# A pause in the gathers around each block that is selected by one-hots, and the selection moved to the head of its step

## What is computed

```
x_i, x_j = x[dst], x[src]
h = relu(concat(x_i, x_j - x_i) @ W1 + b1)     # 64
h = relu(h @ W2 + b2)                          # 128
h = relu(h @ W3 + b3)                          # 64
m = h @ W4 + b4                                # 32
s, cnt = segment_sum(m, dst), segment_sum(1, dst)
out = layernorm(x + s / max(cnt, 1))
```

## Time and profile before

| what | value |
|---|---|
| median of 3 runs | 2409.53 us (2392.46 to 2433.17) |
| profiled execution, span | 2441.1 us |
| TensorE (PE) busy, 13131 matmul records | 1767.5 us, 72% |
| weight loads (PEld) | 1040.0 us |
| VectorE busy | 947.9 us, 39% |
| ScalarE busy | 602.6 us, 25% |
| GpSimd (POOL) busy | 1125.9 us, 46% |
| DMA | 283.06 MB, mean 116 GB/s |

### The profile page before, as it was taken

How to read it: one execution, slowest core, us unless ns; L and a number is a source line. 1 busy time by engine, 2 the same in 40 slices (tenths; PEclk the granted TensorE clock), 3 DMA queues, 4 the chain that set the end, 5 groups by cost and what they waited for, 6 DMA issues and landing times.

```text
span 2441.1 us, 39243 instructions
## 1 busy us (share of the span) xinstructions
PE 1767.5 (72%) x13131; PEld 1040.0 (43%) x13131; DVE 947.9 (39%) x3086; ACT 602.6 (25%) x945; POOL 1125.9 (46%) x1165
## 2 busy tenths in 40 slices
PE   3133777777768777878787778786867778777797
PEld 2112444444444444444444444444444444444454
DVE  3663343333333343333333333443333333333356
ACT  2233122222212222212222222222221222122234
POOL 5275444453544454354545454544444454444411
PEclk7555787877878787777778877777877877787888
DMA  5334643343434443353434353544344344444332
GB/s 128 98 93 88 200 112 112 106 140 94 136 101 116 126 121 109 103 147 91 135 105 136 104 152 92 152 109 114 104 123 115 111 114 109 133 118 118 109 106 59
DMA packets 189929, 283.06 MB, mean 116 GB/s; under 512 B 84614, under 2 KB 90169, under 8 KB 189156
## 3 DMA queue, kind: packets, MB, share of 16 engines
q1 hardware_dynamic: 152341, 241.67, 33.7%
q0 software_dynamic: 36704, 37.00, 7.3%
q10 hardware_dynamic: 682, 1.85, 0.3%
HBM read 266.51 MB, written 13.73 MB: 115 GB/s over the span
## 4 chain that ended last, share of the span: by engine, by line
PE 63%; issue 23%; another core or an unknown queue 6%; DVE 3%; ACT 2%; DMA 1%; SPq 1%; DVEq 0%; POOL 0%; ACTq 0%; POOLq 0%
PE ps L964 22%; PE ps L996 12%; PE ps L988 10%; PE ps L1019 5%; PE ps L1004 4%; PE ps L919 3%; PE ps L901 3%; PE ps L1016 2%; PE ps L978 2%; ACT work L716 1%; ACT work L731 1%; DMA sums<-in_src 1%; DVE region L1410 0%; DVE region L1292 0%
## 5 line engine op out<-in xcount | busy, mean ns | idle before, releaser
L585 POOL DMA_INDIRECT xj<-z_rows,src_t x1107 | 1074.5, 971 | 1190.9 <-PE ps L919 787.7
L964 PE MATMUL ps<-region,x_p 128*96 128x150 bf16 (+53 forms) x5876 | 569.6, 243 | 416.6 <-issue 407.2
L964 PEld LDWEIGHTS ps<-region,x_p 128*96 128x96 bf16 x5876 | 440.6, 142 | 572.9 <-issue 566.7
L731 ACT ACTIVATE work<-ps,b3s 128x512 f32<-128x512 f32 x196 | 134.7, 687 | 1335.5 <-PE ps L996 1037.1
L996 PE MATMUL ps<-work,w3s 128*64 128x512 f32 x784 | 356.6, 840 | 21.2 <-issue 21.1
L1377 DVE TENSOR_SCALAR region<-region,cst 128x1565 bf16<-128x1565 int16 (+6 forms) x416 | 245.7, 634 | 268.0 <-remote 256.3
L988 PE MATMUL ps<-work,w2s 64*128 64x512 f32 x784 | 298.1, 827 | 6.8 <-ACT work L716 5.6
L724 ACT ACTIVATE work<-ps,b2s 128x512 f32<-128x512 f32 x392 | 250.7, 684 | 161.0 <-PE ps L988 82.7
L1392 DVE COPY work<-ps 128x512 f32<-128x512 f32 x194 | 133.4, 687 | 336.4 <-PE ps L1004 217.0
L1386 DVE CAST work<-ps 96x512 bf16<-96x512 f32 x52 | 35.7, 686 | 513.9 <-PE ps L964 506.8
L1410 DVE TENSOR_SCALAR region<-iota_g,dst_rel 128x42 f32<-128x42 f32 x1120 | 185.7, 250 | 0.0
(11 more groups left out here) (156 smaller groups left out, 826.3 us busy)
## 6 DMA issues: line engine op xcount, KB each, us to landing
dstb<-dst_rows SPq DMA_DIRECT2D x196, 252.0 KB
region<-src_rows SPq DMA_DIRECT2D x104, 391.2 KB
region<-src_rows SPq DMA_DIRECT2D x52, 407.2 KB
region<-src_rows SPq DMA_DIRECT2D x52, 403.2 KB
region<-src_rows SPq DMA_DIRECT2D x52, 376.2 KB
region<-src_rows SPq DMA_DIRECT2D x52, 375.8 KB
region<-src_rows SPq DMA_DIRECT2D x52, 374.0 KB
region<-src_rows SPq DMA_DIRECT2D x52, 366.2 KB
```

Source lines behind the costliest of these rows:

```text
L585: pool.indirect_dma_start(out=xj[:, u, j % UT, j // UT, 0:w], out_offset=None, in_=rows, in_offset=bass.IndirectOffsetOnAxis(ap=cols[:, j: ...
L964: chosen = nc.tensor.matmul(ps[0:XP, XBANK[h], lo - h * UE:hi - h * UE], xb[:, a, :], hot[:, q % QN, at + lo:at + hi], start=not begun[h], ...
```

## The change

A constant `QUIET_LEAD = 1` and a semaphore `s_quiet` are new. `quiet_before(g)` lists the sorted blocks before whose selection GpSimd must stop ahead of batch g: those whose step comes when all batches but one of those issued are used. There GpSimd raises `s_quiet` and waits until all eight chunks of the block are selected. TensorE waits for `s_quiet` before the first matmul of the block, and selects all three parts at the head of the sorted step. The first sorted step is step 11 instead of 7. The steps in which VectorE builds the one-hots and SP loads the lists, and the five and eight buffers, stay.

```diff
--- before.py
+++ after.py
@@ -46,8 +46,9 @@
 LISTS = 2 * SBL * T + 2 * LC
 STEPS = []
 AHEAD = 4
+QUIET_LEAD = 1
 HALF_STEP, PARTS_STEP = 0, 1
-FIRST_SORTED, LAST_SORTED = AHEAD + 3, S_N - 8
+FIRST_SORTED, LAST_SORTED = AHEAD + 7, S_N - 8
 SORTED_AT = [FIRST_SORTED + k * (LAST_SORTED - FIRST_SORTED) // (SB - 1) for k in range(SB)]
 for n in range(S_N):
     k = sum(1 for at in SORTED_AT if at < n)
@@ -290,6 +291,7 @@
                                           sem("windows_of_sources_stored"))
         s_masked, s_maskT, s_maskc = sem("sorted_dst_masked"), sem("sorted_dst_transposed"), sem("sorted_dst_copied")
         s_hot, s_block, s_unit0 = sem("source_onehots"), sem("chunks_selected"), sem("unit0_selected")
+        s_quiet = sem("gathers_paused")
         s_turned = sem("rows_transposed")
         s_x2 = sem("x_in_once_more")
         s_l1 = [sem(f"layer1_unit{n}") for n in range(2)]
@@ -374,6 +376,10 @@
 
         def piece(h):
             return slice(h * NC // XH, (h + 1) * NC // XH)
+
+        def quiet_before(g):
+
+            return [STEPS[s] for s in SSTEP if s - STEPS[s] + QUIET_LEAD == g]
 
         def end_of_pass(eng, off):
             eng.sem_inc(s_arrive, 1)
@@ -574,7 +580,13 @@
             nc.gpsimd.memset(zpad[:, :], 0.0).then_inc(s_set, 1)
             nc.gpsimd.memset(w4s[:, :], 0.0).then_inc(s_w4z, 1)
 
+            def stay_quiet(b):
+                pool.sem_inc(s_quiet, 1)
+                pool.wait_ge(s_block, CN * (b + 1))
+
             def gather(g):
+                for b in quiet_before(g):
+                    stay_quiet(b)
                 u, cols = g % R, src_t[:, g * PT:(g + 1) * PT]
                 rows, w = (x, D) if g < PLAIN else (z_rows, H1)
                 if g == PLAIN:
@@ -948,6 +960,8 @@
                     if b:
                         pe.wait_ge(s_xc[1], b)
                     begun[0] = begun[1] = False
+                if piece == 0:
+                    pe.wait_ge(s_quiet, b + 1)
                 if b == 0 and piece == 0:
                     pe.wait_ge(s_xb, 16)
                     pe.wait_ge(s_maskc, 1)
@@ -1028,7 +1042,8 @@
             def step(s):
                 if s < S_N:
                     if is_sorted(s):
-                        selected_x(s, 2)
+                        for k in range(len(PIECES)):
+                            selected_x(s, k)
                     elif is_plain(s):
                         plain_x(s)
                     else:
@@ -1039,9 +1054,6 @@
                 stay_busy({S_N: 4, S_N + 1: 2, S_N + 2: 8}.get(s, 0))
                 if s >= 3:
                     sum_window(s - 3)
-                for lead in (1, 2):
-                    if s >= AHEAD and s + lead < S_N and is_sorted(s + lead):
-                        selected_x(s + lead, 2 - lead)
                 if s < S_N and is_sorted(s):
                     selected_layer1(s)
                 if 1 <= s <= S_N:
```

## The result

The changed kernel takes **2731.12 us** (median of 4 runs, 2729.76 to 2738.88); the kernel before, run beside it, 2413.97 us (4 runs, 2392.46 to 2433.17). The ratio is **1.133, 95% interval 1.128 to 1.138**: slower by 13%. The forecast was 2630 us, 9% slower, range 2310 to 2780; the time lies inside, 101 us above the forecast. The profiled execution has a span of 2730.2 us, mean clock 0.757.

A forecast was written before the change was run, and what follows sets the result against it. TensorE was taken as the bound, partly with nothing to start beside gathers. Terms 250 + 1040 + 1255 + 84 + 35 = 2664 us, less 31.6, gave about 2630 us, 9% slower, range 2310 to 2780.

The forecast's parts named there:

- Long stretches starve every engine: Beside 20 and 30 us of unbroken gathers TensorE runs only 72 and 77 matmuls, leaving 34 and 63 for afterwards.
- the row of 16 gathers: Unbroken gathers in the old profile, 1677.21 to 1697.11: TensorE starts 54 matmuls in 6.4 us, then 18 in 13.5 us.
- The first rival: In long gather stretches TensorE keeps two matmuls per us, the 16 gathers being a special case: 2200 to 2360 us; chance 0.22.
- the one where the effects cancel: Rival: cycles near 36 and 47 us, 2360 to 2455 us in all; chance 0.14.
- tail: From the last layer 2 to the end of the run: 35.4 us, unchanged.
- profile to median: The old profile's span lay 31.6 us above the median of the runs, so 31.6 us were taken off the sum.
- The left-over time: Matmuls left after a stretch, with restart (2.7 us) and late clock (2.3 us): 9.5 us per three-step cycle, 13.3 per four-step.
- The selection: All 113 matmuls at the sorted step's head: 8.7 us with late one-hots, plus 0.3 for semaphores, 9.0 us per cycle.
- The start: From the run's start to the first selection's end: 250 us, bounds 240 and 262.
- The end: After the last selection: 43 gathers with about 88 matmuls beside them, then 188 matmuls left, 84 us in all.
- The upper bound: Left-over matmuls at half clock, 4 us restart, 10 us selection: cycles of 44 and 59 us, near 2960 us in all.
- The rule that fetch is hidden: Instruction fetch is hidden because the sequencer dispatches more slowly than fetch fills; the prediction said the trace does not agree.

The follow-up runs named there:

- e2: The changed kernel with GpSimd also waiting after every four gathers until these have landed: 2288 us, 0.951 of the kernel before.
- g3: The changed kernel with a rest of fixed length for GpSimd ahead of every batch of eight gathers: 2262 us, 0.909 of the kernel before.
- f1: The kernel before with a rest of fixed length (three clearings) for GpSimd ahead of every four gathers: 2016 us, 0.811 of the kernel before.
- e1: The changed kernel without GpSimd's pause and TensorE's wait for it, the selection still whole at the head: 2396 us, 0.996 of the kernel before.
- e4: The changed kernel with QUIET_LEAD = 3 instead of 1: 2714 us, 1.127 of the kernel before.
- f2: The changed kernel, pause kept, with a rest of fixed length for GpSimd ahead of every four gathers: 2266 us, 0.910 of the kernel before.
- f4: As f2, but without GpSimd's pause and TensorE's wait for it: 2027 us, 0.816 of the kernel before.
- e3: The kernel before with GpSimd also waiting after every four gathers until these have landed: 2355 us, 0.979 of the kernel before.
- m1: The kernel before with each gather replaced by GpSimd clearings about as long, plus a rest before each: 1622 us in one run.

## Why the prediction was right, and where it missed

**Long stretches starve every engine: right.** It was the row of 16 gathers against the rival that called it a special case. In 30 us of gathers I gave TensorE 77 matmuls and it ran 79; in 20 us I gave 72 and it ran 78. Left over were to be 63 and 34 matmuls: measured 62 and 28. The model behind these numbers, one matmul per 2.1 us to the end of a stretch, was wrong: TensorE comes as far as the transposes that need ScalarE's next result, some 78 matmuls, and 10 us more of gathers bring one. That 77 came so near to 79 is in part luck; behind the last selection the same model gave 88 beside 53.6 us, and 78 ran. e2, g3 and f1 show the cause, since breaking the stretches takes the loss away, and e1 that the pause makes the stretches. The first rival (2200 to 2360) and the one where the effects cancel fall with the cycles.

**The sum, term by term**, from the first selection's end to the span's:

| term | forecast | measured |
|---|---|---|
| first selection done | 250 | 263.5 |
| 27 cycles of three steps | 38.5 each | 38.9 |
| 24 cycles of four steps | 52.3 each | 53.7 |
| all cycles | 2295 | 2339 |
| last selection to last layer 2 | 84 | 92.4 |
| tail | 35.4 | 35.4 |
| sum | 2664 | 2730.2 |
| profile to median | - 31.6 | + 0.9 |

The cycles are means here, from one selection's end to the next, so that they add up; the medians above (38.2 and 54.4) go from row transposes to row transposes.

The first and the last selection's end, and the last layer 2, in order of time:

```profile
261.76 1.70 PE L978 MATMUL ps<-region,x_p 128*96 128x144 bf16 x29 [1.11 <-DVE region L1389]
...
2600.76 1.71 PE L978 MATMUL ps<-region,x_p 128*96 128x144 bf16 x29 [0.20 <-DVE region L1389]
...
2693.70 1.13 PE L1002 MATMUL ps<-work,w2s 64*128 64x512 f32 x4
```

- *The left-over time was mis-sized for long stretches.* In cycles of three steps it is 9.8 us (787.35 to 797.18) against 9.5 forecast; in cycles of four 17.1 us (742.63 to 759.74) against 13.3. The count of matmuls was right, the restart was not: 5.0 us instead of 2.7. I took 2.7 us from a place where TensorE itself had work at hand; here TensorE stands at L1018 for a ScalarE that was starved for 17.56 us and has to be fed first. My upper bound of 4 us had this reason, and I did not take it. The rest of the 3.8 us is the clock, at half until about 754: 17.1 less 5.0 and the 8.3 us of the matmuls leaves 3.8 us for it against my 2.3. Over the whole trace the left-over time is 10.4 and 16.75 us on the mean; 0.9 x 27 and 3.45 x 24 are 107 us.
- *The selection was mis-sized the other way.* I took 9.0 us with the hand-over; it takes 8.35 us in cycles of three (mostly 7.9 at L978) and 7.15 in cycles of four, on the mean. VectorE's one-hots are late by 1.28 us, and by 0.2 to 0.5 us at the end of a cycle of four, not by 2. That gives back 0.65 x 27 + 1.85 x 24 = 62 us, so that the cycles as a whole missed by 44 only: two errors of opposite sign, which is luck and not accuracy.
- *The start* missed by 13.5 us, just outside my bounds (240 to 262): I counted SP's queue at nothing, and in it the rows of destinations come late. VectorE and TensorE in order of time:

```profile
237.86 0.49 DVE L1381 TENSOR_SCALAR region<-dstb,node_off 126x1024 bf16<-126x1024 int16 x1 [8.21 <-DMA dstb<-dst_rows]
```

```profile
238.49 0.64 PE L913 MATMUL ps<-region,ywin 126*64 126x512 bf16 x2 [5.99 <-DVE region L1381]
```

  TensorE's wait is 6.0 of the 13.5 us. No run tests why that load came late, and the other 7.5 us stay open.
- *The end*, 92.4 instead of 84 us: beside the last 43 gathers TensorE ran 78 matmuls and not 88, and started again 7.7 us after them (2656.30 to 2664.05) and not 2.7.
- *The upper bound was added up wrong.* With its own terms a cycle of four takes 30 + 10 + 19 + 4 = 63 us and not 59, so it lies near 3060 us and not 2960. The range is also given in three ways (2460 to 2900, 2480 to 2780, 2310 to 2780). The time lies inside each, so nothing hangs on it here.
- *Profile to median.* The kernel before had been profiled in an execution 31.6 us above its median; I took that off a sum whose terms were mostly lengths read inside cycles. The changed kernel's profiled span is within 1 us of its median. That is a third of the 101 us.

**The signs.** Seen: selections of 113 matmuls in 7 to 9 us (I had said 8 to 10) without "issue", 52 pauses, stretches of 20 and 30 us, the idle time moved to L1018 and L1002, and "PE" waiting for ScalarE. Wrong: the clock, 0.757 where I said under 0.75. The 4-step cycle has 0.75, but the 3-step one 0.82, and the selection now runs at 2.4 GHz throughout (2.41 + 2.69 + 1.72 us of clean parts, here 4.95 + 1.71). Wrong too: "some 50 matmuls fast, then two per us, then less"; it was 39 in the first 6.4 us, 40 more in bursts, then none. TensorE waited for gathered rows for 20.1 us only (L931), and e4 shows that there was nothing to save. VectorE's one-hots never held TensorE for over 3 us.

**The rule that fetch is hidden** (the Trainium skill, "Runtime: NRT & Kernel Launch", section "Instruction fetch mechanics"). The prediction took the low pace beside gathers for a case against it. That reading does not hold: TensorE is slow there, but nothing shows that it waits for a fetch. The trace records the packets that bring instructions. Queue q8 has 108 of 16 KB, one per about 256 of TensorE's matmuls and weight loads. In the stretch of 30 us one comes at 711.73 and the next at 752.39, after TensorE has started again at 747.59; behind the last selection one comes at 2599.68 and the next at 2666.14, after the start at 2664.05. In 37 of the 51 stretches between selections none comes between the first 6.4 us and the restart. The second queue of this kind, q14, has none between 688.00 and 748.04, and ScalarE starts again at 746.85; behind the last selection it has one at 2659.67, before ScalarE's start at 2663.31. So a stop can end without such a packet, and a late fetch is not shown as its cause.

**What the rivals had right.** The prediction priced the pause as the maker of long stretches only. f2 against f4 shows a second price, hidden while starvation bounds: 0.910 against 0.816, since GpSimd's pauses and stretches add up.

## What to carry to other kernels

When "issue" stands in front of one engine beside another engine's indirect DMAs, look at how long those run without a break, and at what the engine gets done beside them: here some 40 to 50 matmuls at full pace and about 78 in all, then nothing, as ScalarE had stopped. Break the long runs rather than synchronise around the victim; a rest of about 2 us after every four gathers made this kernel 19% faster, while a pause that protected one piece of work made 20 and 30 us stretches of the rest and cost 13%. Price a new wait by the longest uninterrupted stretch that it makes, and the restart by the engine that is last to be fed.

## What the runs showed of the hardware

- Beside unbroken gathers TensorE, ScalarE and VectorE slow down (40 matmuls, 4 activations and 10 VectorE operations in 23.4 us) and then stop: no matmul and no activation in 28.0 us. ScalarE starts 5 activations and TensorE, which then waits for it, about 78 matmuls beside 20, 30 or 53.6 us of gathers. ScalarE comes back 2.8, 4.2 and 7.0 us after the last gather. A break of about 2 us carries TensorE through the next 5 us, one of 1.3 us does not quite (115.7 us of "issue" against 9.4).
- The landing of four gathers, waited for by GpSimd, took 3.1 us on average and up to 7.9 (e3), though the last gather's own time is 0.94 us.
- VectorE's one-hots take 862 ns each in m1 beside GpSimd's constant clearing, 634 ns in the kernel before. In f1, with a clearing in a quarter of the time, 668 ns. The row of m1's page:

```profile
L1390 DVE TENSOR_SCALAR region<-region,cst 128x1565 bf16<-128x1565 int16 (+6 forms) x416 | 337.3, 862 | 11.8 <-DMA region<-src_rows 10.8
```

- The kernel before took 2406 us on one chip and 2476 to 2487 us on three others, 3% apart; e2 and g3 stand on different chips, so their difference (0.951 and 0.909) is less sure than the intervals say.
